# Causal attention: GpSimd takes up to 9 of 16 tiles of exponentials into a partial sum, and rows of constants are loaded where they are used

## The chip, the cores and the metric

One Trainium2 chip, one core. The metric is the device time of one execution in microseconds. The kernel is one program that runs two transformer layers: about twenty phases one after the other, each ending in a barrier of all engines.

## What is computed

```
x = x + L0_xattn(layernorm(x), ctx)      # 16 heads of 16, keys: 1601 rows of ctx
x = x + L0_ffn(layernorm(x))             # 32 experts, capacity 80, and 16 small adapters
x = x + L1_xattn(layernorm(x), ctx)
x = x + L1_ffn(layernorm(x))             # 16 experts, top 4, and 2 shared ones

L1_xattn:  x = ln1(xx);  x = x + mha(x, x, causal=True);  x = ln2(x);  x = x + mha(x, ctx, causal=False)

mha(x, y): q, k, v = projections of ln(x), ln(y), ln(y)         # 16 heads of 32, 2048 queries
    a = softmax(q k^T / sqrt(32))
    if causal:  a = a * (t > s)          # key t, query s: AFTER the softmax, later keys are kept
    x_out = x + (a v) li1_w + li1_b
    return x_out + gelu(ln(x_out) li2_w + li2_b) li3_w + li3_b
```

Since the mask is applied after the softmax, every key counts in the divisor, but only keys later than the query count in the values.

## The kernel before, in words

`program` runs the phases in order: `load_constants` (all small constants, among them `rows`, 2832 numbers that are broadcast to the 128 partitions by one DMA), `ctx_block`, `layernorm`, `attention`, `project_out`, router and experts of the first layer, then the second layer: `layernorm` (twice with a gain and an offset from `rows`), `attention_stacked` (the causal one, `a1`, and later the one over ctx, `a2`), `project_out`, `gelu_ffn`, and at the end `half_rows`, `gate1`, `route` and `moe`. The profile writes both attentions of the second layer with the same names (`a_e`, `a_pd`); they are told apart by time: the tile loop of the causal one runs from about 1378 to 2340 us of the span, that of the other from about 2650 to 3444.

`attention_stacked` goes over 4 groups of 4 heads and, in each, over 4 chunks `qc` of 512 queries: 16 chunks `n`. In a chunk it goes over tiles `kt` of 128 keys (16 in a1, 13 in a2). In a1 the tiles with `kt < 4 qc` are "passed": all their keys are earlier than the queries, so they only need the sum of exponentials, which ScalarE accumulates (L1031). The others are active: 16, 12, 8 and 4 in the four chunks. The first four active tiles (`i` = 0 to 3) are the diagonal ones. For each tile and each of the 4 heads:

- TensorE computes the scores (`score`, L1185 or L1182) into one of 3 PSUM tiles `sc`;
- ScalarE writes the exponentials `e` (L1034) into a ring of `ering` buffers, 3 in a1 and 4 in a2;
- in a diagonal tile GpSimd multiplies one 128x128 block per head by the mask, into `em` (L992), and `po` waits for it (`masked`);
- TensorE adds the values into `po` (`sum_values`, L1208, L1211, L1212) and, by a matmul with ones, the divisors into `pd` (`sum_weights`, L1229). Each f32 matmul is two instructions in the profile, so the 4 heads of a tile are 8.

TensorE runs a tile behind: in iteration m it does scores 0 and 1 of tile m, `sum_values` of tile m-1, scores 2 and 3 of tile m, `sum_weights` of tile m-1. Between these steps it puts "units" of the next chunk (`some_work`): 64 matmuls for the row maxima, which VectorE reduces (L1154, L1082, three PSUM tiles `wb` in turn), projections of q, k and v, and the division of the chunk before. The number of units by step is fixed in advance, in proportion to `TILE_WORK` 8 and `PASSED_WORK` 5.

In a2, GpSimd adds 8 of the 13 tiles of exponentials of a chunk (L999) into `part_sum`, cleared at the start of the chunk by a memset (L982); TensorE leaves out `pd` for those and adds `part_sum` by one such matmul set at the last tile (L1226). ScalarE doesn't write a buffer of the ring before GpSimd has added what was in it (`part_added`). In a1 GpSimd only makes `em`.

Engines take their instructions in order. The SP queue issues nearly all DMAs. At the end of `half_rows` it issues 16 loads for `wall` (L2006), the weights of the routed experts, that `moe` uses; the phase doesn't wait for them. In `gate1` VectorE starts with a memset and then the sum of the scores and `gate_bias` (L1927); `route` begins with the store of `meta` (L2124), which the phase waits for.

Of the kernel before, what the change touches and what calls it, by code (L numbers as in the profile page):

```python
# [100 lines left out]
def load_constants(nc, a, cols, rows, ident, ones, x_sb):  # L101
    ctx, sb, ps, sem = phase(nc, "init")
    with ctx:
# [20 lines left out]
def layernorm(nc, name, src, dst, rows, width, affine=None, outs=(), ident=None):  # L124
# [6 lines left out]
    with ctx:  # L131
# [4 lines left out]
        eps = sb("eps", [P, 1])  # L136
        tp = ps("tp", [P, 4, CH]) if outs else None
# [6 lines left out]
        groups = [(k, t0, min(t0 + TPC, n)) for t0 in range(0, n, TPC) for k in range(nk)]  # L144

        @block.vector
        def _(dve):
# [8 lines left out]
            if affine is not None:  # L156

                dve.wait_ge(var_ready, n)
                for t in range(n):
                    dve.scalar_tensor_tensor(out=dst[:, t, :], in0=src[:, t, :], scalar=mv[:, t, 0:1], in1=affine[0],  # L160
                                             op0=ALU.subtract, op1=ALU.mult).then_inc(scaled, 1)
# [4 lines left out]
            for t in range(n):  # L166
# [4 lines left out]
                else:  # L171
                    dve.wait_ge(scaled, t + 1)
                    dve.scalar_tensor_tensor(out=dst[:, t, :], in0=dst[:, t, :], scalar=rstd[:, t:t + 1], in1=affine[1],
# [623 lines left out]
def attention_stacked(nc, a, name, wq, wk, wv, xq, nkq, xk, nkk, nkeys, scale, causal, ot, ones, bq=None, bk=None, bv=None, ering=4, ones_at=None):  # L797
# [57 lines left out]
    for m in range(nkt * NC):  # L855
# [3 lines left out]
    shared = [[kt for kt in range(1, nkt - 2) if kt % 4 and own_sum and not causal]  # L859
              for n in range(NC)]  # L860
# [10 lines left out]
    for n in range(NC):  # L871
# [12 lines left out]
        during.append(work)  # L884
    after = [(u, n) for n in (NC - 2, NC - 1) for u in ("divisors", "divide")]
# [4 lines left out]
    with ctx:  # L890
# [10 lines left out]
        part_sum = sb("part_sum", [P, HG, CH]) if own_sum and not causal else None  # L901
# [23 lines left out]
        o_taken, inverse_spread, part_added, part_cleared = sem("o_taken"), sem("inverse_spread"), sem("part_added"), sem("part_cleared")  # L925
# [41 lines left out]
        def _(pool):  # L967
# [9 lines left out]
            for n in range(NC if causal or own_sum else 0):  # L977
# [3 lines left out]
                if not causal:  # L981
                    pool.memset(part_sum[:, :, :], 0.0).then_inc(part_cleared, 1)  # L982
                    pool.wait_ge(part_cleared, n + 1)
                for kt in range(nkt):
# [9 lines left out]
                    if kt in shared[n]:  # L994
                        m = nshared[n] + shared[n].index(kt)
                        pool.wait_ge(exp_done, HG * (nkt * n + kt + 1))
                        if m:
                            pool.wait_ge(part_added, m)
                        pool.tensor_tensor(part_sum[:, :, :], part_sum[:, :, :], e[:, (nkt * n + kt) % ering, :, :],  # L999
                                           ALU.add).then_inc(part_added, 1)  # L1000

        @block.scalar
        def _(act):
# [10 lines left out]
            for m in range(nkt * NC):  # L1014
                r = kt_rows[m % nkt]
                for j in range(HG):
                    act.wait_ge(sc_ready, HG * m + j + 1)

                    if m >= ering:
# [3 lines left out]
                        if kt in shared[n]:  # L1023
                            act.wait_ge(part_added, nshared[n] + shared[n].index(kt) + 1)
# [95 lines left out]
        def _(pe):  # L1120
# [67 lines left out]
            def sum_values(n, kt):  # L1188
# [14 lines left out]
                for j in range(HG):  # L1203
# [8 lines left out]
                    pe.matmul(po[h:h + SLOT, P * i:P * i + P], w, em[:r, kt % 2, j, :], start=(i == 0), stop=stop)  # L1212
# [3 lines left out]
            def sum_weights(n, kt):  # L1216
# [5 lines left out]
                if kt == nkt - 1 and not causal:  # L1222
                    pe.wait_ge(part_added, nshared[n + 1])
# [8 lines left out]

            for u in before:
# [6 lines left out]
            shares = [1, 1, 1, 1, 1, 1 if own_sum else 0]  # L1240
            tile_work = [PASSED_WORK if passed(m // nkt, m % nkt) else TILE_WORK for m in range(nkt * NC + 1)]
            for m in range(nkt * NC + 1):
                n, kt = m // nkt, m % nkt
                ahead = (m + LEAD) // nkt
                window = range(max(nkt * ahead - LEAD, 0), min(nkt * (ahead + 1) - LEAD, nkt * NC + 1))
                work = during[ahead] if ahead < NC else []
                in_all = sum(shares) * sum(tile_work[k] for k in window)

                def some_work(step):

                    before_tile = sum(shares) * sum(tile_work[k] for k in range(window.start, m))
                    lo, hi = (-(-len(work) * (before_tile + tile_work[m] * sum(shares[:i])) // in_all) for i in (step, step + 1))
                    for u in work[lo:hi]:
                        unit(u)

# [3 lines left out]
                for half in range(2):  # L1259
                    if n < NC:  # L1260
                        score(n, kt, 2 * half)
                    some_work(3 * half)
                    if n < NC:
                        score(n, kt, 2 * half + 1)
                    some_work(3 * half + 1)
# [4 lines left out]
                    some_work(3 * half + 2)  # L1270
# [4 lines left out]
def project_out(nc, name, ot, wo_dram, bias, res, dst):  # L1275

    ctx, sb, ps, sem = phase(nc, name)
    with ctx:
        wo = sb("wo", [P, NG, D])
        y = [ps(f"y{i}", [P, D]) for i in range(4)]  # L1280
        w_loaded, y_ready, summed, biased = sem("w_loaded"), sem("y_ready"), sem("summed"), sem("biased")
        block = ctx.enter_context(nc.Block())

        @block.sync
        def _(sp):
            sp.dma_start(wo[:, :, :], wo_dram).then_inc(w_loaded, 16)

# [17 lines left out]
        def _(pool):  # L1305
            for t in range(NT):
                pool.wait_ge(summed, t + 1)
                pool.tensor_tensor(dst[:, t, :], dst[:, t, :], bias, ALU.add).then_inc(biased, 1)


def gelu_ffn(nc, a, name, xt, w2_dram, w3_dram, b2, b3, xo, adds, dst, halved):
# [9 lines left out]
    with ctx:  # L1321
        w2 = sb("w2", [P, KC, FF])
        w3 = sb("w3", [P, nj, D])
# [1394 lines left out]
```

## Time and profile before

| | us |
|---|---|
| time, median of 3 runs | 4138.86 (4130.42 to 4160.15) |
| time of the profiled execution | 4170.53 |
| its span | 4168.8 |
| busy: TensorE matmul | 3451.8 (83%) |
| busy: VectorE | 2533.2 (61%) |
| busy: ScalarE | 1936.3 (46%) |
| busy: GpSimd | 1257.1 (30%) |
| mean granted clock of TensorE | 0.899 |

Times in the rows are microseconds from the start of the span unless marked ns. A row of a timeline is an instruction or a run of equal ones: start, length, engine, line, operation, output <- inputs, count, and in brackets the idle time before it and what ended that. PE is TensorE, PEld its weight loads, DVE VectorE, ACT ScalarE, POOL GpSimd, SPq the queue of SyncE. Averages over the whole span hide the stages: the two attention loops of the second layer, 1756 us of it, are another matter than the phases between them.

### The profile page before, as it was taken

The page shows a single profiled execution, that of the slowest core. Times are in us where ns is not written, and L with a number is a line of the kernel's source. Part 1 is how long each engine was busy: PE and PEld are TensorE (multiplying, and loading weights), DVE is VectorE, ACT ScalarE, POOL GpSimd, SP SyncE. Part 2 cuts the span into 40 slices and gives each one's busy share as a digit, 9 for nine tenths or more (in the row PEclk, how much of TensorE's full clock was granted, in tenths as well). Part 3 has the DMA queues.
Part 4 walks back from the last instruction along what each step waited for, and adds up shares of the span by engine and source line. Part 5 has one row for each costly group of instructions (what it writes and reads, how often), then busy time and mean ns, then how long its engine had stood idle before and what let it go on. Part 6 is the DMA issues. An engine that isn't in the chain of part 4 may idle for free. (4 is left out here: it accounts for less than half of the span.)

```text
span 4168.8 us, 66056 instructions
## 1 busy us (share of the span) xinstructions
PE 3451.8 (83%) x23063; PEld 1585.2 (38%) x23063; DVE 2533.2 (61%) x4809; ACT 1936.3 (46%) x3897; POOL 1257.1 (30%) x658
## 2 busy tenths in 40 slices
PE   4999999518855999999999773899999994838997
PEld 1333333307752232333322442233333323526775
DVE  4777774481135777687776245777777744344564
ACT  1677777001101456565666361355555561512442
POOL 2000000102211000010000161377777783524454
PEclk7999999758876999999999786899999996968998
DMA  1000000336641000000000061100000001562445
GB/s 59 10 16 10 11 7 3 102 118 208 223 150 38 21 8 16 14 11 19 9 6 4 6 193 50 24 11 21 10 21 9 9 1 54 185 245 82 89 83 116
DMA packets 174222, 236.69 MB, mean 57 GB/s; under 512 B 36499, under 2 KB 148442, under 8 KB 166874
## 3 DMA queue, kind: packets, MB, share of 16 engines
q1 hardware_dynamic: 154858, 207.81, 15.9%
q0 software_dynamic: 19056, 24.88, 3.3%
q8 instruction: 179, 2.93, 0.3%
q14 instruction: 129, 1.06, 0.1%
HBM read 136.16 MB, written 66.82 MB: 49 GB/s over the span
## 5 line engine op out<-in xcount | busy, mean ns | idle before, releaser
L1082 DVE TENSOR_REDUCE a_part_max<-a_wb 128x1 f32<-128x512 f32 (+1 forms) x2048 | 1168.3, 626 | 300.7 <-PE a_wb L1154 291.6
L1034 ACT ACTIVATE a_e<-a_sc 128x512 f32<-128x512 f32 (+1 forms) x1472 | 798.1, 598 | 803.3 <-PE a_sc L1185 800.2
L1154 PE MATMUL a_wb<-a_ks,a_qs 96*128 96x512 f16 (+1 forms) x2048 | 746.2, 372 | 48.4 <-DMA a_qs<-a_stage 28.0
L999 POOL TENSOR_TENSOR a_part_sum<-a_part_sum,a_e 128x2048 f32<-128x2048 f32 x128 | 581.4, 4542 | 141.2 <-ACT a_e L1034 78.0
L1185 PE MATMUL a_sc<-a_qs,a_ks 97*128 97x512 f16 (+1 forms) x1472 | 546.0, 384 | 12.9 <-DMA a_qs<-a_neg_max 8.1
L607 DVE TENSOR_REDUCE xa_part_max<-xa_mx 128x2 f32<-128x802 f32 x512 | 472.1, 986 | 131.3 <-PE xa_mx L711 128.3
L543 ACT ACTIVATE xa_e<-xa_sc 128x512 f32<-128x512 f32 (+1 forms) x832 | 445.6, 596 | 128.0 <-PE xa_sc L698 120.4
L1154 PEld LDWEIGHTS a_wb<-a_ks,a_qs 96*128 96x128 f16 x2048 | 200.0, 98 | 657.3 <-DVE a_part_max L1082 473.3
L992 POOL TENSOR_TENSOR a_em<-a_e,a_later 128x512 f32<-128x512 f32 x64 | 81.1, 1267 | 955.1 <-ACT a_e L1034 944.9
L1208 PE MATMUL a_po<-a_e,a_v 128*32 128x512 f32 (+1 forms) x2432 | 323.9, 605 | 1.8 <-ACT a_dc L1012 1.0
L734 PE MATMUL xa_po<-xa_e,xa_v 128*32 128x256 f32 (+1 forms) x3328 | 269.6, 396 | 7.5 <-ACT xa_oc L593 2.6
L1229 PE MATMUL a_pd<-a_e,ones 128*32 128x512 f32 (+1 forms) x1920 | 257.9, 609 | 0.0
L1031 ACT ACTIVATE a_e<-a_sc 128x512 f32<-128x512 f32 x384 | 223.4, 648 | 28.3 <-PE a_sc L1182 27.4
L1185 PEld LDWEIGHTS a_sc<-a_qs,a_ks 97*128 97x128 f16 (+1 forms) x1472 | 145.0, 100 | 204.7 <-ACT a_e L1034 87.2
L711 PE MATMUL xa_mx<-xa_khi,xa_qhi 32*128 32x401 f16 x1024 | 180.7, 352 | 18.5 <-DVE xa_part_max L607 13.9
L2288 POOL DMA_INDIRECT routed_sums<-moe_ye,moe_ids x79 | 139.3, 1763 | 164.9 <-DVE moe_ye L2427 119.2
L698 PE MATMUL xa_sc<-xa_qs,xa_ks 49*128 49x512 f16 (+1 forms) x832 | 177.2, 394 | 12.2 <-DMA xa_qs<-xa_neg_max 12.2
L2327 PE MATMUL moe_g<-wall,moe_xt 128*128 (+1 forms) x666 | 173.1, 317 | 1.5 <-ACT moe_xt L2379 0.8
L2327 PE MATMUL moe_up<-wall,moe_xt 128*128 (+1 forms) x666 | 171.5, 316 | 1.6 <-issue 1.6
L1182 PE MATMUL a_sc<-a_ks,a_qs 97*128 97x512 f16 x384 | 146.6, 404 | 7.4 <-ACT a_e L1031 6.6
L2346 PE MATMUL moe_y<-wall,moe_ht 128*128 (+1 forms) x999 | 129.2, 275 | 26.9 <-DVE moe_ht L2405 26.3
L2395 DVE TENSOR_TENSOR moe_hf<-moe_sg,moe_up 128x352 f32<-128x352 f32 x111 | 57.9, 521 | 136.9 <-ACT moe_sg L2367 111.7
(348 smaller groups left out, 4458.2 us busy)
## 6 DMA issues: line engine op xcount, KB each, us to landing
experts_w_up<-in_we SPq DMA_DIRECT2D x32, 1024.0 KB, 7.1
a_ffn_stage<-in_wm SPq DMA_DIRECT2D x72, 272.0 KB, 3.5
expert_halves<-a_ffn_cut SPq DMA_DIRECT2D x72, 272.0 KB, 3.1
wall<-expert_halves SPq DMA_DIRECT2D x18, 1088.0 KB, 19.4
experts_w_down<-in_we SPq DMA_DIRECT2D x32, 512.0 KB
a_qs<-a_stage SPq DMA_DIRECT2D x384, 32.0 KB, 1.8
moe_xr<-sorted_rows SPq DMA_DIRECT2D x79, 136.5 KB
a_ks<-a_stage SPq DMA_DIRECT2D x336, 32.0 KB, 1.8
```

The lines of the kernel that those rows point to most:

```text
L543: act.activation(e[:r, m % ering, j, :], src[:r, :], ACT.Exp, scale=scale).then_inc(s_taken, 1)
L607: dve.tensor_reduce(part_max[:, 2 * h:2 * h + 2, t, c], src[:, :, :mxw], AX.X, ALU.max).then_inc(m_taken, 1)
L734: last = pe.matmul(po[h:h + SLOT, q], w, e[:r, m % ering, j, q], start=(kt == first and part == 0), stop=stop)
L999: pool.tensor_tensor(part_sum[:, :, :], part_sum[:, :, :], e[:, (nkt * n + kt) % ering, :, :], ALU.add).then_inc(part_added, 1)
L1031: act.activation(e[:, m % ering, j, :], sc[(HG * m + j) % NSC][:, :], ACT.Exp, scale=scale, accum_out=span_sum[:, n % 2, t, j, c:c + 1]).t ...
L1034: act.activation(e[:r, m % ering, j, :], sc[(HG * m + j) % NSC][:r, :], ACT.Exp, scale=scale).then_inc(exp_done, 1)
L1082: dve.tensor_reduce(part_max[:, j, t, k:k + 1], src[:, :mxw], AX.X, ALU.max).then_inc(unit_taken, 1)
L1154: last = pe.matmul(dst[:, :mxw], qs[:STACK, j, n % NQ, P * t:P * t + P], ks[:STACK, g % 2, j, mxs[k]:mxs[k] + mxw], start=True, stop=True)
L1185: pe.matmul(sc[i % NSC][:r, :], ks[:STACK + 1, n // NCH % 2, j, P * kt:P * kt + r], qs[:STACK + 1, j, n % NQ, :], start=True, stop=True).t ...
L1208: last = pe.matmul(po[h:h + SLOT, :], w, e[:r, m % ering, j, :], start=(kt == first), stop=stop)
L1229: last = pe.matmul(pd[h:h + SLOT, :], ones[:r, :SLOT], e[:r, m % ering, j, :], start=(kt == first), stop=(kt == nkt - 1))
L2327: last = pe.matmul(dst[:, :], xt[j % 2][:, px, k, :], weights(u, pw, off + EI * k, EI), start=(k == 0 and px == 0 and pw == 0), stop=(k == ...
```

## The change

Four things:

- In a1 GpSimd also adds tiles of exponentials: those active tiles with `i > 0`, `i % 3 != 0` and `kt < nkt - 2`, in chunks with more than 4 active tiles. This is 9, 6, 4 and 0 tiles in the four chunks of a group, 76 in all. TensorE leaves out `pd` for them and adds `part_sum` once in each of the 12 chunks that have any. The ring in a1 stays at 3 buffers. In program order GpSimd makes the mask of a tile first and then adds that tile.
- In both attentions the memset of `part_sum` goes: the first shared tile of a chunk is copied, not added. The tiles of a2 are the same as before.
- To make room for `part_sum` in a1, `rows` no longer stays in SBUF. Each phase that needs a part of it loads it itself, on SP: `ctx_block` (bv, waited for at its end), `layernorm` with a gain, `project_out`, `gelu_ffn` (behind w2 and w3), `gate1`.
- `some_work` is rewritten (`work_at`) and gives each step the same units as before.

```diff
+def row_of(a, n):
+    o, k = ROWS[n]
+    return a["rows"][:, o:o + k].partition_broadcast(P).rearrange("p o n -> p (o n)")
...
-            sp.dma_start(rows[:, :], a["rows"].partition_broadcast(P).rearrange("p o n -> p (o n)")).then_inc(loaded, 16)
             sp.dma_start(x_sb[:, :, :], a["x"].rearrange("o (t p) d -> p (o t) d", p=P)).then_inc(loaded, 16)
-            sp.wait_ge(loaded, 48)
+            sp.wait_ge(loaded, 32)
...
+        if affine is not None:
+            @block.sync
+            def _(sp):
+                for i in range(2):
+                    sp.dma_start(gains[i][:, :], affine[i]).then_inc(gains_loaded, 16)
...
                 dve.wait_ge(var_ready, n)
+                dve.wait_ge(gains_loaded, 32)
...
-    shared = [[kt for kt in range(1, nkt - 2) if kt % 4 and own_sum and not causal]
-              for n in range(NC)]
+    def adds_up(n, kt):
+
+        i = kt - (TPC * (n % NCH) if causal else 0)
+        active = nkt - (kt - i)
+        return own_sum and active > TPC and 0 < i and kt < nkt - 2 and (i % 3 != 0 if causal else kt % 4 != 0)
+
+    shared = [[kt for kt in range(nkt) if adds_up(n, kt)] for n in range(NC)]
...
-                if not causal:
-                    pool.memset(part_sum[:, :, :], 0.0).then_inc(part_cleared, 1)
-                    pool.wait_ge(part_cleared, n + 1)
...
                         pool.wait_ge(exp_done, HG * (nkt * n + kt + 1))
+                        tile = e[:, (nkt * n + kt) % ering, :, :]
                         if m:
-                            pool.wait_ge(part_added, m)
-                        pool.tensor_tensor(part_sum[:, :, :], part_sum[:, :, :], e[:, (nkt * n + kt) % ering, :, :],
-                                           ALU.add).then_inc(part_added, 1)
+                            pool.wait_ge(pool_added, m)
+                        if kt == shared[n][0]:
+                            pool.tensor_copy(part_sum[:, :, :], tile).then_inc(pool_added, 1)
+                        else:
+                            pool.tensor_tensor(part_sum[:, :, :], part_sum[:, :, :], tile, ALU.add).then_inc(pool_added, 1)
...
-                if kt == nkt - 1 and not causal:
-                    pe.wait_ge(part_added, nshared[n + 1])
+                if kt == nkt - 1 and shared[n]:
+                    pe.wait_ge(pool_added, nshared[n + 1])
                     for j in range(HG):
                         h = SLOT * j
                         pe.matmul(pd[h:h + SLOT, :], ones[:, :SLOT], part_sum[:, j, :], start=False, stop=False)
...
             sp.dma_start(wo[:, :, :], wo_dram).then_inc(w_loaded, 16)
+            sp.dma_start(bias[:, :], bias_dram).then_inc(bias_loaded, 16)
...
             sp.dma_start(w2[:, :, :], w2_dram).then_inc(w2_loaded, 16)
             sp.dma_start(w3[:, :, :], w3_dram).then_inc(w3_loaded, 16)
+            sp.dma_start(b3[:, :], b3_dram).then_inc(b3_loaded, 16)
...
+        @block.sync
+        def _(sp):
+            sp.dma_start(gate_bias[:, :], bias_dram).then_inc(bias_loaded, 16)
...
             dve.wait_ge(iota_ready, 2)
-            link(dve.tensor_tensor(sfc[:, :, :], sco[:, :, :], gate_bias.unsqueeze(1).to_broadcast([P, NT, E1]), ALU.add))
+            dve.wait_ge(bias_loaded, 16)
+            link(dve.tensor_tensor(sfc[:, :, :], sco[:, :, :], gate_bias[:, :].unsqueeze(1).to_broadcast([P, NT, E1]), ALU.add))
...
             sp.dma_start(ct[:, 0, :], a["ctx_t"]).then_inc(loaded, 16)
-            sp.wait_ge(loaded, 16)
+            sp.dma_start(bv[:, :], row_of(a, "bv0")).then_inc(loaded, 16)
+            sp.wait_ge(loaded, 32)
```

## Rows read from the trace of the kernel before

**Rows 1.** Busy time by stretch: span and length, each engine's busy us, granted clock, DMA.

```profile
1624.50:1695.40 70.90, 69.28 (x438) 20.30 (x437) 47.58 (x78) 36.26 (x72) 4.58 (x4) 1.00 0.08 22
1763.30:1818.00 54.70, 52.55 (x308) 16.87 (x306) 46.33 (x79) 37.43 (x100) 5.06 (x4) 1.00 0.03 8
```

**Rows 2.** Timeline, one plain tile of a 16-tile chunk of the causal attention.

```profile
1645.54 1.06 PE L1229 MATMUL a_pd<-a_e,ones 128*32 128x512 f32 x8
1646.54 0.39 PE L1185 MATMUL a_sc<-a_qs,a_ks 97*128 97x512 f16 x1
...
1647.51 1.06 PE L1208 MATMUL a_po<-a_e,a_v 128*32 128x512 f32 x8
...
1649.15 1.09 ACT L1034 ACTIVATE a_e<-a_sc 128x512 f32<-128x512 f32 x2 [1.11 <-PE a_sc L1185]
...
1651.45 1.06 PE L1208 MATMUL a_po<-a_e,a_v 128*32 128x512 f32 x8
```

**Rows 3.** Groups by line and shape (busy us, mean ns): causal loop, then the other.

```profile
L1082 DVE TENSOR_REDUCE a_part_max<-a_wb 128x1 f32<-128x512 f32 x960 | 606.7, 685 | 149.4 <-PE a_wb L1154 145.5
...
L1082 DVE TENSOR_REDUCE a_part_max<-a_wb 128x1 f32<-128x401 f32 x960 | 492.0, 568 | 125.1 <-PE a_wb L1154 120.6
```

**Rows 4.** Groups by line, whole span: what operations cost on GpSimd.

```profile
L999 POOL TENSOR_TENSOR a_part_sum<-a_part_sum,a_e 128x2048 f32<-128x2048 f32 x128 | 581.4, 4542 | 141.2 <-ACT a_e L1034 78.0 <-issue 49.1 <-POOL a_part_sum L999 0.4
...
L982 POOL MEMSET a_part_sum<- 128x2048 f32 x16 | 28.9, 1806 | 104.8 <-PE a_pd L1229 104.7
L1374 POOL TENSOR_TENSOR a_xo<-a_xo,x 128x4096 f32<-128x4096 f32 x3 | 27.8, 9256 | 45.6 <-POOLq L2616 27.2 <-POOLq L131 18.4
...
L485 POOL CAST xa_qhi<-xa_raw 128x512 f16<-128x512 f32 x16 | 9.8, 611 | 428.5 <-ACT xa_raw L555 421.1 <-DMA xa_ks<-xa_khi 7.4
```

**Rows 5.** Timeline, diagonal tiles: a 16-tile chunk, then one of 8 active tiles.

```profile
1629.03 1.27 POOL L992 TENSOR_TENSOR a_em<-a_e,a_later 128x512 f32<-128x512 f32 x1 [3.76 <-ACT a_e L1034]
...
1632.85 1.27 POOL L992 TENSOR_TENSOR a_em<-a_e,a_later 128x512 f32<-128x512 f32 x1 [2.55 <-ACT a_e L1034]
...
1638.70 0.87 PE L1211 MATMUL a_po<-a_e,a_v 128*32 128x384 f32 x8
...
1790.51 1.27 POOL L992 TENSOR_TENSOR a_em<-a_e,a_later 128x512 f32<-128x512 f32 x1 [2.55 <-ACT a_e L1034]
...
1796.11 0.88 PE L1211 MATMUL a_po<-a_e,a_v 128*32 128x384 f32 x8
```

**Rows 6.** Timeline, the last chunk of the second attention.

```profile
3404.95 37.26 POOL L999 TENSOR_TENSOR a_part_sum<-a_part_sum,a_e 128x2048 f32<-128x2048 f32 x8 [2.04 <-issue]
...
3442.26 1.06 PE L1226 MATMUL a_pd<-a_part_sum,ones 128*32 128x512 f32 x8 [3.51 <-POOL a_part_sum L999]
```

**Rows 7.** DMA issues: count, KB each, median us from issue to landing.

```profile
x<-token_sums SPq DMA_DIRECT2D x2, 2048.0 KB, 8.5
...
x<-in_x SPq DMA_DIRECT2D x1, 2048.0 KB, 12.5
...
ct<-in_ctx_t SPq DMA_DIRECT2D x1, 800.5 KB, 4.2
```

**Rows 8.** Around gate1: SP's issues, VectorE's first use of gate_bias, DMA load, one landing.

```profile
3676.70 20.38 SPq L2006 DMA_DIRECT2D wall<-expert_halves  x16
...
3698.44 0.43 DVE L1927 TENSOR_TENSOR gate_sfc<-m_sco,rows 128x256 f32<-128x256 f32 x1 [0.59 <-POOL meta L1920]
...
3714.94 0.37 SPq L2124 DMA_DIRECT2D token_halves<-meta  x1
3726.80 104.51 SPq L2249 DMA_DIRECT2D moe_xr<-token_halves  x16
...
3720.00:3721.00 1.00, 0.00 (x0) 0.00 (x0) 0.93 (x8) 0.00 (x0) 0.00 (x0) 0.50 1.00 418
3722.00:3723.00 1.00, 0.00 (x0) 0.00 (x0) 0.86 (x5) 0.00 (x0) 0.00 (x0) 0.50 0.97 62
...
token_halves<-meta SPq DMA_DIRECT2D x1, 136.0 KB, 10.9
```

More of the change, by code:

```diff
@@ L98, in phase, with load_constants @@
     return ctx, sb, ps, sem
-def load_constants(nc, a, cols, rows, ident, ones, x_sb):
+def row_of(a, n):
+    o, k = ROWS[n]
+    return a["rows"][:, o:o + k].partition_broadcast(P).rearrange("p o n -> p (o n)")
+def load_constants(nc, a, cols, ident, ones, x_sb):
     ctx, sb, ps, sem = phase(nc, "init")
@@ L136, in layernorm @@
         eps = sb("eps", [P, 1])
+        gains = [sb(f"gain{i}", [P, width]) for i in range(2)] if affine is not None else None
+        gains_loaded = sem("gains_loaded")
         tp = ps("tp", [P, 4, CH]) if outs else None
@@ L884, in attention_stacked, with work_at @@
         during.append(work)
+    shares = [1, 1, 1, 1, 1, 1 if own_sum else 0]
+    tile_work = [PASSED_WORK if passed(m // nkt, m % nkt) else TILE_WORK for m in range(nkt * NC + 1)]
+    def work_at(m, step):
+        ahead = (m + LEAD) // nkt
+        window = range(max(nkt * ahead - LEAD, 0), min(nkt * (ahead + 1) - LEAD, nkt * NC + 1))
+        work = during[ahead] if ahead < NC else []
+        in_all = sum(shares) * sum(tile_work[k] for k in window)
+        before_tile = sum(shares) * sum(tile_work[k] for k in range(window.start, m))
+        lo, hi = (-(-len(work) * (before_tile + tile_work[m] * sum(shares[:i])) // in_all) for i in (step, step + 1))
+        return work[lo:hi]
     after = [(u, n) for n in (NC - 2, NC - 1) for u in ("divisors", "divide")]
@@ L900, in attention_stacked @@
         later = sb("later", [P, P]) if causal else None
-        part_sum = sb("part_sum", [P, HG, CH]) if own_sum and not causal else None
+        part_sum = sb("part_sum", [P, HG, CH]) if own_sum else None
         part_max = sb("part_max", [P, HG, TPC, nmx])
@@ L1023, in _ @@
                         if kt in shared[n]:
-                            act.wait_ge(part_added, nshared[n] + shared[n].index(kt) + 1)
+                            act.wait_ge(pool_added, nshared[n] + shared[n].index(kt) + 1)
                     n, kt = m // nkt, m % nkt
@@ L1211, in sum_values @@
                         pe.matmul(po[h:h + SLOT, :P * i], w, e[:r, m % ering, j, :P * i], start=False, stop=False)
-                    pe.matmul(po[h:h + SLOT, P * i:P * i + P], w, em[:r, kt % 2, j, :], start=(i == 0), stop=stop)
+                    last = pe.matmul(po[h:h + SLOT, P * i:P * i + P], w, em[:r, kt % 2, j, :], start=(i == 0), stop=stop)
                 if not own_sum or kt in shared[n]:
@@ L1231, in sum_weights, with some_work @@
                 last.then_inc(pv_done, 1)
+            def some_work(m, step):
+                for u in work_at(m, step):
+                    unit(u)
             for u in before:
@@ L1269, in _, with project_out @@
                         sum_weights((m - 1) // nkt, (m - 1) % nkt)
[L1270 removed]
+                    some_work(m, 3 * half + 2)
             for u in after:
                 unit(u)
[L1275 removed]
+def project_out(nc, name, ot, wo_dram, bias_dram, res, dst):
     ctx, sb, ps, sem = phase(nc, name)
@@ L1305, in _, with gelu_ffn @@
         def _(pool):
+            pool.wait_ge(bias_loaded, 16)
             for t in range(NT):
                 pool.wait_ge(summed, t + 1)
-                pool.tensor_tensor(dst[:, t, :], dst[:, t, :], bias, ALU.add).then_inc(biased, 1)
-def gelu_ffn(nc, a, name, xt, w2_dram, w3_dram, b2, b3, xo, adds, dst, halved):
+                pool.tensor_tensor(dst[:, t, :], dst[:, t, :], bias[:, :], ALU.add).then_inc(biased, 1)
+def gelu_ffn(nc, a, name, xt, w2_dram, w3_dram, b2, b3_dram, xo, adds, dst, halved):
     ctx, sb, ps, sem = phase(nc, name)
@@ L1892, in _, with gate1 @@
             pair(NP - 1, last=True)
-def gate1(nc, a, sco, gate_bias, meta):
+def gate1(nc, a, sco, bias_dram, meta):
     ctx, sb, ps, sem = phase(nc, "gate1")
@@ L2482, in program @@
         a["ident"] = ident
-        load_constants(nc, a, cols, rows, ident, ones, x)
+        load_constants(nc, a, cols, ident, ones, x)
         def col(n):
@@ L2487, in col @@
             return cols[:, o:o + k]
-        def row(n):
-            o, k = ROWS[n]
-            return rows[:, o:o + k]
         def scope():
@@ L2595, in program, with ctx_block @@
                 half_rows(nc, a, x, sco, wall, wall_in, half_ident, before, every, ident)
-                gate1(nc, a, sco, row("gate_bias"), meta)
+                gate1(nc, a, sco, row_of(a, "gate_bias"), meta)
             route(nc, a, meta, slots, tile_e, before, every)
             moe(nc, a, wall, wall_in, slots, tile_e, half_ident, x, out)
-def ctx_block(nc, a, name, ct):
+def ctx_block(nc, a, name, ct, bv):
     ctx, sb, ps, sem = phase(nc, name)
```

49 lines of the change are left out of this document (22 added, 27 removed).

## The prediction

> **What bounds the kernel now.** I read the page first (shares, then the chain, which covers only the tail of the program), then busy time by stretch, then the timeline of single tiles. [Rows 1] cut one head group of the causal attention into its chunks of 512 queries: in the chunk with 16 active tiles TensorE is busy 69.3 of 70.9 us, in the one with 8 it is 52.6 of 54.7, at a granted clock of 1.00 (the 2.4 GHz level), while VectorE is at 47.6 and 46.3 and GpSimd at 4.6 and 5.1. So TensorE sets the pace, and GpSimd is idle. VectorE is the next bound: 46.3 of 54.7 us in the chunk with 8 active tiles.
>
> [Rows 2] show one steady tile: the two value sums (po) stand 3.94 us apart (1647.51, 1651.45), packed with matmuls. The divisor sum (pd) begins at 1645.54 and the next matmul at 1646.54: a pd costs 1.00 us of TensorE. The tile's last exponential ends at 1649.15 + 1.09 = 1650.24, and po for it begins at 1651.45. Without the pd between them po would begin at 1650.45, 0.2 us after the exponential: just enough. So a dropped pd is worth its full 1.00 us in a plain tile.
>
> **What is removed and added in the causal attention.** By the new rule GpSimd takes 9, 6, 4 and 0 tiles of a group's four chunks, 19 per group, 76 in all. Removed: 76 pd. Added: a sum over part_sum in 12 chunks, 1.00 us each. Naively 76 - 12 = 64 us. Two things take from this.
>
> Plain tiles (diagonal index i of 4 or more): 7, 4 and 2 per group, 52 in all. Every three tiles hold two adds of 4.54 us [rows 4], 9.1 us of GpSimd, against 3 x 3.94 - 2 x 1.00 = 9.8 us of TensorE. The ring of three exponential buffers gives an add until about half a microsecond into the third tile after its own. The second add of a pair begins at latest 4.5 us after the first and ends 9.1 us after the first pair's exponential, about 1.5 us before its buffer is wanted. VectorE needs 4 to 5 reductions of 0.685 us at most a tile [rows 3], 2.7 to 3.4 us, against 2.9 to 3.0 us of TensorE in a shared tile; the three work buffers and the unshared tile between take up that excess. I give these 52 tiles 1.00 us each: -52.
>
> Diagonal tiles (i = 0 to 3): here GpSimd also makes em, the masked block, and po waits for it. GpSimd works in order, so the mask of tile 3 queues behind the add of tile 2. In [rows 5] mask 2 of a 16-tile chunk begins at 1632.85, as soon as its exponentials are done; the pd of tile 1 comes after these, so its removal makes nothing earlier. Then: mask 1.27, add 4.54, mask 1.27, some 0.1 of signals: po of tile 3 not before 1632.85 + 7.2 = 1640.05. Before it began at 1638.70. So up to po 3 nothing is gained from the two dropped pd and 1.35 us are lost. The chunk with 8 active tiles: 1790.51 + 7.2 = 1797.7 against 1796.11, a loss of 1.6; I take 1.6 for the 12-tile chunk too. Four groups: 4 x (1.35 + 1.6 + 1.6) = 18. After po 3 everything follows from it.
>
> Causal attention: -52 + 12 + 18 = -22 us.
>
> The first operation of a chunk is a copy of 128x2048, not an add. No such row exists. Bounds: the memset of the same tile, 1.81 us, and the add, 4.54; nearest is the cast of 128x512, 0.61, four times that is 2.4 [rows 4]. I take 2.2. Mask 1 begins at 1629.03 and ends at 1630.30, so the copy ends at 1632.5, before mask 2 wants GpSimd at 1632.85: free. Any longer copy delays mask 2 one to one; at 4.54 it is 2.0 us late, in 12 chunks 24 us. The Trainium skill (GPSIMD Engine Reference, Engine selection) has one-input operations at roughly line rate and two-input ones about twice slower, by which the copy is hidden; no row here shows that copy.
>
> **Second attention.** Memset and its wait go, and the first add becomes a copy. Only the last chunk, which has no maxima to compute, waits for GpSimd: its adds start at 3404.95, when the second tile's exponentials are ready, run without a gap, and the sum over part_sum follows at 3442.26 [rows 6]. The memset was done before; the copy saves 4.54 - 2.2 = 2.3 us. -2.4 with the small waits for it (0 to -5).
>
> **Rows of constants.** At the start x lands 12.5 us after its issue, queued with the 1416 KB of constants. The same 2048 KB alone took 8.5 us [rows 7]: -4.0. The next block gains 256 KB for bv beside the 800.5 KB of ct (4.2 us): at that rate at most +1.3, taken as +1. The layernorm gains are loaded under 16 statistics instructions, the output biases behind the weights that TensorE waits for longer, b3 under the first full-width add on GpSimd, 9.26 us [rows 4]: nothing, and if a cover were gone, about 2 us each.
>
> The gate's bias is another matter. It is issued on SP at the start of gate1, and SP has just issued 16 transfers for wall, one expert each [rows 8]. These are still running: 418 GB/s with the DMA engines full until 3721, then 62 GB/s at 3722. The precedent is meta, 136 KB, issued at 3714.94: it landed 10.9 us later, at 3725.8, and small packets appear only when the large ones have ended. So this queue works in order, and 16 numbers per partition issued at about 3697.9 land at about 3722.5. VectorE's first instruction that wants them ran at 3698.44: +24 us (23 to 26). Behind it lie the whole gate chain and route, up to the first loads of moe at 3726.80; the chain from meta to there is VectorE's, so it isn't shortened by meta now landing sooner. The Trainium skill (DMA: Bandwidth & Descriptors, Queues, rings and completion order) says that each DMA engine consumes a ring's descriptors in order; the rows of meta agree.
>
> **Sum.** -22 - 2.4 - 3 + 24 = -3.4 us. The profiled execution took 4170.53 us (span 4168.8), 0.8% above the median of 4138.86; the stages concerned are the same, so I take the difference over: 4138.86 - 3.4 = 4135 us.
>
> **Rivals.**
> - The bias isn't held up (it lands within 2 us, as if on a queue of its own): +1.4 in place of +24, so 4113 us. For it: the transfer is tiny. Against: meta.
> - The diagonal costs nothing and all 64 us come: 4135 - 42 = 4093 us, faster by 1.1%. It would need a mask that isn't behind an add; the program order of GpSimd says otherwise.
> - The copy is as slow as an add: +24 from mask 2, 4159 us. For it: no row of a copy. Against: the cast.
> - Slower: GpSimd becomes the bound through the ring of three. With an add of a us, a pair of shared tiles costs 2a in place of 9.8 from a = 4.9 on, 26 pairs, and the diagonal 12 x (a - 4.54). At a = 5.9 this is 26 x 2.0 + 12 x 1.36 = 68 us: 4203 us; slower by 1% from a = 5.5. Against: in the second attention 128 adds beside a busy VectorE held 4.54 us, and VectorE's reductions there took 0.568 us for 401 columns, in the causal one 0.685 for 512 [rows 3], the same per column within 6%. The Trainium skill (GPSIMD Engine Reference, Key points) names contention with VectorE instructions that have two SBUF inputs; this rival is that rule, and the rows of VectorE here are nearly all reductions from PSUM.
>
> **How the numbers follow.** Forecast 0.62, bias free 0.10, all 64 us 0.06, slow copy 0.13, slow add 0.05, the rest 0.04 for small effects either way. The range reaches from the free bias with a few microseconds more to the slow copy with as many: 4105 to 4168. About 1%, 41 us, is what a measurement can tell from no change: faster 0.06, same 0.89, slower 0.05. The chief claim is that two effects of some 25 us cancel.
>
> **What would show it.** In the causal chunks: a gap on TensorE before po of tile 3 with GpSimd's mask as its releaser, mask 3 beginning 5.8 us after mask 2; tile steps of 2.95 us where pd is gone; adds of 4.5 us; a copy of 1.8 to 2.5 us. Chunks of 16 active tiles shorter by some 5 us, of 12 by 1, of 8 longer by 0.6. In gate1: VectorE waiting some 24 us for the DMA of gate_bias. At the start: statistics 3 us earlier. The forecast is wrong if the bias lands at once, if TensorE waits for exponentials after the dropped pd (margin 0.2 us), or if the clock falls below 1.00 after the gaps at tile 3.

## The result, and the profile after

The changed kernel takes 4217.98 us (median of 4 runs, 4208.73 to 4239.58), the kernel before in the same comparison 4137.43: a ratio of 1.019, 95% interval 1.015 to 1.023, that is 80.5 us slower. I had forecast 4135 us, no change. The profiled execution of the changed kernel has a span of 4207.0 us, at a mean granted clock of 0.889.

The path can be cut where `a_dc`, the copy of a chunk's divisors, starts: once per chunk, 16 per attention. View of one tile (`a_dc`), in a window for each attention; the columns are count, duration in ns (least, median, greatest), first and last start in us. The kernel before:

```profile
L1012 ACT ACTIVATE a_dc<-a_pd x16: 591/591/592, 1450.3 to 2340.4; 128x512 f32<-128x512 f32 x16
L1012 ACT ACTIVATE a_dc<-a_pd x16: 591/591/592, 2705.2 to 3451.1; 128x512 f32<-128x512 f32 x16
```

The changed kernel:

```profile
L1044 ACT ACTIVATE a_dc<-a_pd x16: 592/592/592, 1435.1 to 2322.1; 128x512 f32<-128x512 f32 x16
L1044 ACT ACTIVATE a_dc<-a_pd x16: 592/592/593, 2686.2 to 3500.6; 128x512 f32<-128x512 f32 x16
```

| stretch | before | after | change | forecast |
|---|---|---|---|---|
| to the first row maximum of the causal attention | 1310.6 | 1301.7 | -8.9 | -3 |
| causal attention, to its last `a_dc` | 1029.8 | 1020.4 | -9.4 | -22 |
| from there to the first `a_dc` of the second attention | 364.8 | 364.1 | -0.7 | 0 |
| second attention, first to last `a_dc` | 745.9 | 814.4 | +68.5 | -2.4 |
| last `a_dc` to the store of `meta` (L2124, now L2160) | 263.8 | 287.5 | +23.6 | +24 |
| from there to the end of the span | 453.9 | 419.0 | -34.8 | 0 |

The last row is not the change. Between its first and last transposition on TensorE, `moe` took 399.4 us in the trace of the kernel before, 365.0 in that of the changed one, and 364.8 to 366.9 in those of all ten experiments, one of them (e2) with the gate and the loads untouched. So it was a stall in the one profiled execution of before, which took 4170.53 us while the median is 4137. Likewise the first row moves by more than the change explains: it lies between 1296.5 and 1331.4 in these traces; of its 8.9 us, 3.5 are there at the first normalised tile. Without both, the stretches give -3.5 - 9.4 - 0.7 + 68.5 + 23.6 = +78.5 us, against +80.5 between the medians.

**Second attention.** Busy time by stretch, first to last `a_dc` (columns as in [rows 1]), before and then after:

```profile
2705.20:3451.10 745.90, 719.37 (x4338) 231.21 (x4336) 511.83 (x1009) 431.70 (x808) 571.84 (x135) 0.99 0.05 11
```

```profile
2686.20:3500.60 814.40, 748.58 (x4338) 240.93 (x4336) 566.34 (x1009) 433.40 (x808) 503.58 (x120) 0.96 0.04 10
```

The same 4338 matmuls; VectorE's time grew by 54.5 us with the same 1009 instructions. The copy that spreads the inverse divisors over 512 columns (`a_spread`, one per chunk) explains it. The tile view of it, second attention, last chunks left out, after:

```profile
L1129 DVE COPY a_spread<-a_inverse x14: 4099/4486/4494, 2695.3 to 3411.0; 128x512 f32<-128x512 f32 x14
```

Before it was 427 to 455 ns. The timelines show why. The changed kernel, GpSimd, then VectorE, then TensorE:

```profile
2690.92 1.89 POOL L1030 COPY a_part_sum<-a_e 128x2048 f32<-128x2048 f32 x1 [14.17 <-ACT a_e L1066]
2694.99 4.52 POOL L1032 TENSOR_TENSOR a_part_sum<-a_part_sum,a_e 128x2048 f32<-128x2048 f32 x1 [2.17 <-ACT a_e L1066]
...
2695.29 4.49 DVE L1129 COPY a_spread<-a_inverse 128x512 f32<-128x512 f32 x1
2699.71 1.52 DVE L1114 TENSOR_REDUCE a_part_max<-a_wb 128x1 f32<-128x401 f32 x3
...
2700.33 0.52 PE L1186 MATMUL a_wb<-a_ks,a_qs 96*128 96x401 f16 x1 [3.07 <-DVE a_part_max L1114]
```

The kernel before, same chunk:

```profile
2709.94 9.21 POOL L999 TENSOR_TENSOR a_part_sum<-a_part_sum,a_e 128x2048 f32<-128x2048 f32 x2 [3.37 <-issue]
...
2714.30 0.45 DVE L1097 COPY a_spread<-a_inverse 128x512 f32<-128x512 f32 x1
```

In the kernel before the copy came 4.36 us after the first add had begun, at its end. Now GpSimd's first operation is a copy of 1.89 us, so the second tile's add can begin as soon as its exponentials are there, 0.30 us ahead of VectorE's copy, and the copy ends 0.27 us after the add. Meanwhile the three work buffers of the maxima fill, and TensorE stands still for 3.07 us. The view of TensorE's waits over the loop and some us more, after (us in total, times, longest):

```profile
PE a_wb L1186 <- DVE a_part_max L1114: 42.8, 20, 3.4
```

It was 1.6 before. After such a gap the clock falls. Busy time by stretch of 4 us, after:

```profile
2690.00:2694.00 4.00, 4.00 (x27) 1.22 (x26) 3.13 (x7) 2.06 (x5) 1.89 (x1) 1.00 0.15 35
2694.00:2698.00 4.00, 3.25 (x23) 1.37 (x21) 3.63 (x4) 2.59 (x5) 3.01 (x1) 1.00 0.19 46
2698.00:2702.00 4.00, 1.67 (x6) 0.95 (x7) 4.00 (x6) 0.60 (x1) 1.52 (x2) 0.75 0.10 26
2702.00:2706.00 4.00, 4.00 (x24) 2.07 (x24) 2.13 (x5) 1.51 (x3) 4.00 (x1) 0.83 0.01 2
2706.00:2710.00 4.00, 4.00 (x27) 0.97 (x25) 3.73 (x8) 2.73 (x6) 0.61 (x2) 1.00 0.00 0
```

A granted clock of 0.75 or 0.83 is a mean of 1.2 and 2.4 GHz. So the 68.5 us are 29 us more for the same matmuls (748.6 - 719.4) and 39 us more in which TensorE stands still (65.8 against 26.5): the waits for maxima grew by 41 (42.8 - 1.6), some others shrank.

VectorE's copy is held in the same way, for less time, in the trace of the kernel before. A chunk of the causal attention, GpSimd making a mask, then VectorE:

```profile
1460.84 1.27 POOL L992 TENSOR_TENSOR a_em<-a_e,a_later 128x512 f32<-128x512 f32 x1 [67.86 <-ACT a_e L1034]
...
1461.56 0.83 DVE L1097 COPY a_spread<-a_inverse 128x512 f32<-128x512 f32 x1
```

Here, and in two chunks more, the copy begins 0.72 us into a mask and takes 0.83 us, to 0.28 us after the mask's end.

**Causal attention.** The diagonal went as forecast. Timeline of a 16-tile chunk, changed kernel (against [rows 5]):

```profile
1618.08 1.27 POOL L1021 TENSOR_TENSOR a_em<-a_e,a_later 128x512 f32<-128x512 f32 x1 [0.72 <-ACT a_e L1066]
1619.30 4.52 POOL L1032 TENSOR_TENSOR a_part_sum<-a_part_sum,a_e 128x2048 f32<-128x2048 f32 x1
1623.77 1.45 POOL L1021 TENSOR_TENSOR a_em<-a_e,a_later 128x512 f32<-128x512 f32 x1
...
1625.37 1.53 PE L1243 MATMUL a_po<-a_e,a_v 128*32 128x384 f32 x8 [2.56 <-POOL a_em L1021]
```

`po` of tile 3 begins 7.29 us after mask 2 (forecast 7.2), mask 3 5.7 us after it (5.8). Over the causal loop TensorE waits for masks:

```profile
PE a_po L1243 <- POOL a_em L1021: 42.5, 27, 2.7
```

against 2.6 us at this line before (L1211). What I had not priced is what follows the gap of 2.56 us:

```profile
1621.00:1625.00 4.00, 1.81 (x13) 1.16 (x11) 3.50 (x7) 2.12 (x4) 4.00 (x2) 0.97 0.19 49
1625.00:1629.00 4.00, 3.63 (x20) 1.19 (x20) 0.94 (x2) 0.60 (x1) 0.22 (x1) 0.50 0.16 43
1629.00:1633.00 4.00, 4.00 (x21) 1.63 (x20) 1.74 (x3) 1.68 (x3) 3.14 (x1) 0.67 0.00 0
1633.00:1637.00 4.00, 4.00 (x27) 1.06 (x26) 2.92 (x5) 2.06 (x4) 2.69 (x2) 1.00 0.00 0
```

0.50 is 1.2 GHz. TensorE's busy time over the causal attention fell from 973.9 to 924.1 us, by 50 and not by the 64 of the dropped matmuls, and its mean granted clock there from 0.96 to 0.94. Chunk by chunk after the first (from one `a_dc` to the next), those of 16 active tiles came out 2.2 to 3.5 us shorter (forecast some 5), those of 12 between 1.7 shorter and 1.3 longer (forecast 1 shorter), those of 8 longer by 0.6 to 2.3 (forecast 0.6).

**The gate.** Timeline of SP and VectorE, changed kernel, and, of its DMA issues, KB and us to landing:

```profile
3725.68 20.34 SPq L2042 DMA_DIRECT2D wall<-expert_halves  x16
3746.51 1.81 SPq L1949 DMA_DIRECT2D gate_gate_bias<-in_rows  x1
...
3771.49 0.42 DVE L1963 TENSOR_TENSOR gate_sfc<-m_sco,gate_gate_bias 128x256 f32<-128x256 f32 x1 [24.71 <-DMA gate_gate_bias<-in_rows]
```

```profile
gate_gate_bias<-in_rows SPq DMA_DIRECT2D x1, 8.0 KB, 24.9
```

8 KB took 24.9 us to land, behind 16 transfers, and VectorE waited 24.71 us. From the first of the 16 issues to VectorE's sum: 21.7 us before [rows 8], 45.8 now, +24.1.

### The profile page after: what moved, and what is told of

Read it like the earlier page. It is cut to its first block and busy times, and to the rows that moved or that the text cites. A ratio compares the mean times of both kernels' runs of the same rounds, so it can differ in the third digit from the quotient of the medians.

```text
span 4207.0 us, 65463 instructions
## 1 busy us (share of the span) xinstructions
PE 3424.6 (81%) x22551; PEld 1590.6 (38%) x22551; DVE 2582.1 (61%) x4809; ACT 1934.3 (46%) x3897; POOL 1494.7 (36%) x718
## 5 line engine op out<-in xcount | busy, mean ns | idle before, releaser
L1032 POOL TENSOR_TENSOR a_part_sum<-a_part_sum,a_e 128x2048 f32<-128x2048 f32 x176 | 796.5, 4525 | 206.4 <-ACT a_e L1066 193.4
L1217 PE MATMUL a_sc<-a_qs,a_ks 97*128 97x512 f16 (+1 forms) x1472 | 556.1, 391 | 11.9 <-DMA a_qs<-a_neg_max 8.0
L1261 PE MATMUL a_pd<-a_e,ones 128*32 128x512 f32 (+1 forms) x1312 | 181.9, 627 | 0.0
L499 POOL CAST xa_qhi<-xa_raw 128x512 f16<-128x512 f32 x16 | 9.8, 610 | 427.9 <-ACT xa_raw L569 420.6
L1030 POOL COPY a_part_sum<-a_e 128x2048 f32<-128x2048 f32 x28 | 52.9, 1890 | 251.4 <-ACT a_e L1066 243.9
```

Of the source, the lines that this page charges most:

```text
L1032: pool.tensor_tensor(part_sum[:, :, :], part_sum[:, :, :], tile, ALU.add).then_inc(pool_added, 1)
L1217: pe.matmul(sc[i % NSC][:r, :], ks[:STACK + 1, n // NCH % 2, j, P * kt:P * kt + r], qs[:STACK + 1, j, n % NQ, :], start=True, stop=True).t ...
L1261: last = pe.matmul(pd[h:h + SLOT, :], ones[:r, :SLOT], e[:r, m % ering, j, :], start=(kt == first), stop=(kt == nkt - 1))
```

## The experiments

Theory A: VectorE's spreading copy is held by a GpSimd add that has begun before it, until that add ends, and the shorter first operation on GpSimd brought this about. Rivals: something else lengthens the second attention (B), GpSimd holds any VectorE instruction with SBUF on both sides (C), or the copy is slow under GpSimd work wherever it begins (H). Theory D: the gate's bias stands behind 16 transfers; rival E: `moe` gives that back. Theory F: the add ahead of mask 3 is what costs the causal attention its gain; rival G: the gain is only moved. All ratios are to the kernel before, run beside each; its median there lies between 4130.64 and 4137.43 us, so a difference between two experiments that were not run together is good to some 7 us.

**e1_a2_memset.** The changed kernel with GpSimd's second attention as before:

```diff
+                if not causal:
+                    pool.memset(part_sum[:, :, :], 0.0).then_inc(part_cleared, 1)
+                    pool.wait_ge(part_cleared, n + 1)
...
-                        if kt == shared[n][0]:
+                        if causal and kt == shared[n][0]:
```

> The changed kernel, but in the second attention GpSimd clears the partial sum and adds its first tile, as in the kernel before. Theory A (in the changed kernel VectorE's copy that spreads the inverse divisors, L1129, starts 0.3 us after a GpSimd add has begun and is held until it ends, 4.35 us instead of 0.44, because the first operation of a chunk is now 1.89 us long instead of 4.5): the copy falls back into the end of the first add and takes 0.45 us, the second attention is 794 us long again instead of some 850, and the kernel takes 4218 - 55 = about 4163 us. Rival B (something else lengthens the second attention: a lower clock, the layout of memory, the sharing in the first attention that precedes it): within 10 us of 4218 us.

Measured: 4144.59 us, ratio 1.002 (0.999 to 1.005): 73 us less than the changed kernel, and 18 less than expected. The second attention's loop takes 748.9 us, 65.5 less, where I had counted only the 55 us of the copies; one of its 16 copies is still held (4.47 us, the others about 0.43). B falls.

**e2_before_copy.** The converse, on the kernel before:

```diff
-                if not causal:
-                    pool.memset(part_sum[:, :, :], 0.0).then_inc(part_cleared, 1)
-                    pool.wait_ge(part_cleared, n + 1)
...
+                        if kt == shared[n][0]:
+                            pool.tensor_copy(part_sum[:, :, :], tile).then_inc(part_added, 1)
+                        else:
```

> The kernel before, with one edit: in the second attention the clearing and first add of the partial sum become a copy. Nothing else of the change. Theory A: this alone moves VectorE's spreading copy under a GpSimd add; it takes over 4 us in 14 chunks and the kernel takes 4137 + 55 = about 4192 us. Rival B: no slower than before, or 2 us faster as I forecast for this part.

Measured: 4201.22 us, ratio 1.016 (1.012 to 1.020), +67 us, 9 more than expected, from 16 GpSimd operations that became 2.65 us shorter each (4.54 to 1.89) and 16 memsets that went. Loop 814.5 us. In this kernel and window:

```profile
L1097 DVE COPY a_spread<-a_inverse x14: 4099/4483/4490, 2712.7 to 3428.2; 128x512 f32<-128x512 f32 x14
```

**e5_spread_reduce.** The changed kernel, with the copy written as a reduction over an axis of length 1:

```diff
-                    dve.tensor_copy(spread[:, :, :, :], inverse[:, :, :].unsqueeze(3).to_broadcast([P, TPC, HG, SLOT])).then_inc(
+                    dve.tensor_reduce(spread[:, :, :, :].rearrange("p t j d -> p (t j) d"),
+                                      inverse[:, :, :].rearrange("p t j -> p (t j)").unsqueeze(2).unsqueeze(3).to_broadcast([P, TPC * HG, SLOT, 1]), AX.X, ALU.max).then_inc(
```

> The changed kernel; the spreading of the inverse divisors stays on VectorE, at the same place, with the same SBUF source and the same 512 numbers written per partition, but as a reduction over an axis of length 1 instead of a copy. GpSimd's work is untouched. Theory A2 (what is held is the copy form; the copy at 427 ns for 512 numbers, 0.83 ns each, is faster than VectorE's reductions at 1.33 ns each, so it runs in a faster mode, and that mode waits for GpSimd): the reduction takes 0.6 to 0.8 us even when a GpSimd add is running, and the kernel takes 4218 - 66 = about 4152 us. Rival C (any VectorE instruction that both reads and writes SBUF is held by a GpSimd add): over 4 us in 14 chunks, and the time stays at 4218.

Measured: 4153.11 us, ratio 1.003 (1.000 to 1.006), 65 us less than the changed kernel. Timeline of it, GpSimd and VectorE:

```profile
2708.74 9.21 POOL L1032 TENSOR_TENSOR a_part_sum<-a_part_sum,a_e 128x2048 f32<-128x2048 f32 x2 [2.17 <-ACT a_e L1066]
...
2709.05 0.69 DVE L1129 TENSOR_REDUCE a_spread<-a_inverse 128x512 f32<-128x512 f32 x1
```

It begins 0.31 us after the add, as the copy did, moves the same bytes, and takes 0.69 us. C falls: what is held is the faster form. The Trainium skill (SBUF — State Buffer, Who interferes with whom) says just this: VectorE's copies can enter a mode that uses the pair of ports it shares with GpSimd, whoever starts first has that pair for its whole instruction, and a reduction on Trainium2 never contends. The traces agree, with 4.49 against 0.69 us.

**e3_spread_recip.** The changed kernel, with one reciprocal in place of the small one and the copy:

```diff
-                    dve.reciprocal(inverse[:, :, :], den).then_inc(unit_taken, 1)
-                    dve.wait_ge(unit_taken, i + 1)
-                    dve.tensor_copy(spread[:, :, :, :], inverse[:, :, :].unsqueeze(3).to_broadcast([P, TPC, HG, SLOT])).then_inc(
-                        inverse_spread, 1)
+                    dve.reciprocal(spread[:, :, :, :], den.unsqueeze(3).to_broadcast([P, TPC, HG, SLOT])).then_inc(inverse_spread, 1)
+                    dve.wait_ge(inverse_spread, n + 1)
+                    dve.sem_inc(unit_taken, 1)
```

> The changed kernel; VectorE makes the spread inverse divisors with one reciprocal that reads the divisors (in PSUM in the second attention) 32 times over and writes 512 numbers, so the copy from SBUF to SBUF (a_spread from a_inverse) is gone. GpSimd's work stays as it is. Theory A (the hold is a matter of that copy's form): the reciprocal isn't held, 0.6 to 1.2 us, the second attention is back at some 795 us, and the kernel takes 4218 - 55 = about 4163 us. Rival C (anything that VectorE runs against a GpSimd add of two operands is held there): the reciprocal takes over 4 us and the time stays at 4218.

Measured: 4252.96 us, ratio 1.030 (1.024 to 1.035), 35 us more than the changed kernel. A miss, but not in C's favour:

```profile
L1127 DVE RECIPROCAL a_spread<-a_wb x20: 3356/3357/3359, 1447.6 to 3545.6; 128x512 f32<-128x512 f32 x20
L1127 DVE RECIPROCAL a_spread<-a_total x12: 3352/3353/3354, 1518.0 to 2380.3; 128x512 f32<-128x512 f32 x12
```

A reciprocal of 512 numbers costs 3.36 us wherever it stands, from PSUM or SBUF, with or without an add beside it: nothing waits, it is slow, 6.6 ns for a number against 1.3 for the reduction. I had guessed 0.6 to 1.2. It does show that the harm needs no hold by GpSimd, only a VectorE instruction of this length: the second attention's loop is 800.6 us, in line with the table below, and the causal one, where the copy was hardly held, is 54 us longer. One thing more differs there: the long instruction itself reads the divisors' work buffer in the second attention, so that buffer comes free later too.

**e9_divisors_2_later, e10_divisors_4_later.** The changed kernel with the divisors' units 2 and 4 places later in the second attention (e9; e10 has 30 in place of 28):

```diff
-            work[26:26], work[32:32] = [("divisors", n - 1)], [("divide", n - 1)]
+            at = 26 if causal else 28
+            work[at:at], work[at + 6:at + 6] = [("divisors", n - 1)], [("divide", n - 1)]
```

> The changed kernel; in the second attention the two units that make the divisors and the division stand 2 places later in TensorE's and VectorE's order of units, each place about 0.72 us (50 us for some 70 units). In the changed kernel the spreading copy begins 0.30 us (or 0.64) after a GpSimd add of 4.52 us has begun and lasts 4.49 us (or 4.17): in both cases it ends 0.27 us after the add. Theory A (it is held until the add that runs ends): begun 1.4 us later it lasts about 3.0 us, VectorE loses 20 us less in 14 chunks, and by the 66 us that 55 us of hold were worth (e1, e5) the kernel takes about 4218 - 24 = 4194 us. Rival H (the copy is slow under any GpSimd activity, by a factor of ten, wherever in the add it begins): still over 4 us, 4218.

> As e9, 4 places later: the copy begins some 3.2 us into the add. Theory A: it lasts 1.3 to 1.9 us, and the kernel takes about 4218 - 48 = 4170 us. Rival H: over 4 us, 4218. If the shift carries the copy past the end of the add into the next one, single copies of over 4 us remain and the time lies between.

Measured: 4196.09 us (ratio 1.016, 1.012 to 1.021) and 4177.45 us (1.011, 1.007 to 1.014). A pair of timeline rows of e9, then of e10:

```profile
2690.69 9.17 POOL L1033 TENSOR_TENSOR a_part_sum<-a_part_sum,a_e 128x2048 f32<-128x2048 f32 x2 [2.17 <-ACT a_e L1067]
2691.80 3.69 DVE L1130 COPY a_spread<-a_inverse 128x512 f32<-128x512 f32 x1
```

```profile
2720.96 9.18 POOL L1033 TENSOR_TENSOR a_part_sum<-a_part_sum,a_e 128x2048 f32<-128x2048 f32 x2 [2.17 <-ACT a_e L1067]
2723.72 2.05 DVE L1130 COPY a_spread<-a_inverse 128x512 f32<-128x512 f32 x1
```

Start after the add's start plus length: 1.11 + 3.69 = 4.80; 2.76 + 2.05 = 4.81; in the changed kernel 0.30 + 4.49 = 4.79 and 0.64 + 4.17 = 4.81; in the kernel before 4.36 + 0.45 = 4.81. Over all 14 chunks of each of these traces, a copy that begins up to 4.38 us into the add ends 4.79 to 4.82 us after the add's start, about 0.28 after its end. H falls. The dose and its effect, second attention, first to last `a_dc`, always 4338 matmuls:

| kernel | `a_spread`, mean us | VectorE busy | TensorE busy | its waits for maxima | loop |
|---|---|---|---|---|---|
| before | 0.44 | 511.8 | 719.4 | 1.3 | 745.9 |
| e5 | 0.69 | 515.3 | 721.4 | 1.6 | 746.2 |
| e10 | 1.81 | 529.9 | 732.3 | 15.4 | 773.2 |
| e9 | 3.06 | 547.2 | 740.6 | 32.1 | 797.4 |
| changed | 4.35 | 566.3 | 748.6 | 42.5 | 814.4 |

(The means are of the 14 copies inside the loop.) VectorE is far from full in all of them; it is the length of one instruction that matters, against three buffers.

**e4_bias_early.** The changed kernel, with the bias loaded in `half_rows` ahead of the 16 transfers:

```diff
             sp.dma_start(gw[:, :, :], a["gw"]).then_inc(gw_loaded, 16)
+            sp.dma_start(gate_bias[:, :], row_of(a, "gate_bias")).then_inc(bias_loaded, 16)
...
-        @block.sync
-        def _(sp):
-            sp.dma_start(gate_bias[:, :], bias_dram).then_inc(bias_loaded, 16)
```

> The changed kernel; the gate's bias is loaded in the block before gate1, behind the gate's weights and ahead of the 16 transfers of expert weights. Theory D (it stands in the changed kernel behind these 16 transfers on one queue, +24.0 us by the two traces): VectorE's gate chain begins 21.7 us after the first of the 16 is issued instead of 46, and the kernel takes 4218 - 24 = 4194 us. Rival E (the gate's delay is made up in moe, whose stretch was 34 us shorter in the trace of the changed kernel than in that of the kernel before, since the weights have then landed): moe grows by as much as the gate shrinks, and the time stays within 8 us of 4218.

Measured: 4190.73 us, ratio 1.011 (1.007 to 1.015), 27 us less than the changed kernel; `moe` 365.4 us. VectorE's sum of this kernel:

```profile
3770.92 0.42 DVE L1957 TENSOR_TENSOR gate_sfc<-m_sco,gate_bias 128x256 f32<-128x256 f32 x1 [0.62 <-POOL meta L1950]
```

D holds, E falls.

**e6_reduce_bias.** The edits of e5 and e4 together.

> e5_spread_reduce with the gate's bias loaded in the block before gate1 (e4_bias_early's edit). If the two costs are independent: 24 to 27 us less than e5, so about 4127 us, under the kernel before by what the causal sharing and the earlier start bring (9 + 3 us). If the copy is held whatever its form: about 4191 us, as in e4.

Measured: 4125.65 us, ratio 0.996 (0.993 to 0.999), 27 us less than e5: the two costs add up, and without them the change is a small gain.

**e7_no_add_before_mask.** e6 with other shared tiles in the causal attention:

```diff
-        return own_sum and active > TPC and 0 < i and kt < nkt - 2 and (i % 3 != 0 if causal else kt % 4 != 0)
+        return own_sum and active > TPC and 0 < i and kt < nkt - 2 and (i % 3 != 2 if causal else kt % 4 != 0)
```

> e6_reduce_bias with another choice of shared tiles in the causal attention: i % 3 != 2 in place of i % 3 != 0, so 1, 3, 4, 6, 7, 9, 10, 12, 13 and no add of tile 2 stands ahead of the mask of tile 3. Still 9 and 6 tiles in the chunks of 16 and 12 active tiles, 3 in place of 4 in those of 8: 4 divisor sums more. Theory F (the add of tile 2 makes TensorE wait 2.6 us before the value sum of tile 3 in 12 chunks, and these gaps bring the granted clock down, 0.96 against 0.98 in the causal loop): 12 x 2.6 - 4 = 27 us less, and up to 14 more from the clock: 4127 - 27 to - 41, 4086 to 4100 us. Rival G (what is gained ahead of tile 3 is lost behind it, since the adds of tiles 3 and 4 now press on the ring of three buffers): within 8 us of e6.

Measured: 4079.13 us, ratio 0.985 (0.980 to 0.991): 46 us less than e6, 56 less than the kernel before, and below the 4086 to 4100 that I expected. F holds, G falls. The same stretch of a 16-tile chunk, mask 2, mask 3, adds:

```profile
1619.51 1.27 POOL L1021 TENSOR_TENSOR a_em<-a_e,a_later 128x512 f32<-128x512 f32 x1 [0.72 <-ACT a_e L1066]
1623.54 1.26 POOL L1021 TENSOR_TENSOR a_em<-a_e,a_later 128x512 f32<-128x512 f32 x1 [2.77 <-ACT a_e L1066]
1624.76 9.21 POOL L1032 TENSOR_TENSOR a_part_sum<-a_part_sum,a_e 128x2048 f32<-128x2048 f32 x2
```

Mask 3 now waits for its exponentials, not for GpSimd. TensorE's waits for masks at that line fall from 42.0 us to

```profile
PE a_po L1244 <- POOL a_em L1021: 11.6, 15, 1.4
```

and its busy time over the causal attention from 925.8 to 917.2 us although it does 4 more divisor sums. Waits -30, sums +4, and the rest of the matmuls -13 at a mean granted clock of 0.95 against 0.94: -39, and the attention went from 1021.8 to 983.3 us in the traces. The remaining 8 us between the medians are not explained; the runs of one kernel spread by more.

**e8_no_causal_sharing.** e6 without the sharing in the causal attention:

```diff
-        return own_sum and active > TPC and 0 < i and kt < nkt - 2 and (i % 3 != 0 if causal else kt % 4 != 0)
+        return own_sum and not causal and active > TPC and 0 < i and kt < nkt - 2 and (i % 3 != 0 if causal else kt % 4 != 0)
```

> e6_reduce_bias without the sharing in the causal attention: GpSimd only makes the masks there, as in the kernel before. By the two traces the sharing as it is written is worth 9.4 us in the causal attention (64 us less of TensorE's work, 40 us more of waits for masks, 14 us more for the same work at a lower clock), so this kernel is 9 us slower than e6, about 4136 us. If I misread the traces and the sharing gains nothing or costs something, it is as fast as e6 or faster.

Measured: 4126.3 us, ratio 0.998 (0.995 to 1.002), the same as e6 within the intervals. In the traces the causal attention is 1030.2 us against 1021.8, the 8 us expected; the medians don't show them. What can be said is that the sharing as it was written is worth between nothing and some 9 us; the choice of tiles in e7 is worth 46 more.

## Why the prediction was wrong

- **Start, -3:** right, 3.5 us at the first normalised tile.
- **Plain tiles, -52, sums +12, diagonal +18, together -22:** the places and the gaps were right: 64 us less work, and the forecast 18 + 24 = 42 us of waiting ahead of the diagonal `po` came as 42.5 - 2.6 = 40. The step that failed is pricing the rest of the matmuls at the old clock. A gap of some 2.6 us can bring 1.2 GHz for several microseconds after it (0.50 and 0.67 of the clock in the rows above); the matmuls that stayed took 14 us longer in all, so -9.4 and not -22. I had named this among what would make the forecast wrong, but put nothing into the sum or the range for it.
- **Copy on GpSimd, 2.2:** 1.89, ahead of mask 2 in time, as forecast; the rival of a slow copy is out. The adds took 4.52 us, so the rival of a slow add is out too. Out are also a bias that lands at once and all 64 us of the dropped sums.
- **Second attention, -2.4:** this step failed, by 71 us. I asked what becomes of GpSimd's own chain, and only in the last chunk, where somebody waits for it. I did not ask what else on the chip depended on when its adds run. The fact was within reach: the copy `a_spread` took 0.43 us for 512 numbers where a reduction of 512 took 0.685 [rows 3], so it ran in a faster mode; it came at the end of an add; and making the first operation 2.65 us shorter would put the next add in front of it. The hold itself was in the trace too, 0.83 us in place of 0.43 beside a mask. My rival of contention with VectorE was dismissed with "the rows of VectorE here are nearly all reductions from PSUM". "Nearly all" was the fault: the exception is one instruction per chunk, and one of 4.4 us against three buffers is enough. The sentence of the Trainium skill that I cited (GPSIMD Engine Reference, Key points) names VectorE instructions in a two-port mode first, and I weighed it only for those with two SBUF inputs, and only for what they do to GpSimd.
- **Gate, +24:** right, 24.1 between the traces, 27 in e4. That small packet behind 16 transfers was visible in the landing of `meta` [rows 8].
- **Profiled time against the median:** I took the difference over; e2's trace shows `moe` at 365 us with the same gate, so the profile of before held a stall of 34 us of its own. It changed nothing in the sum.

The range of 4105 to 4168 was built from the rivals about GpSimd's price and the bias; none of them held a VectorE instruction that waits for GpSimd. With the two missed terms, -3.4 + 71 + 13 = +81, the sum is what was measured.

## What to carry to other kernels

Before giving GpSimd more work, or only other times for its work, list VectorE's SBUF-to-SBUF copies, with how long after the start of a GpSimd operation each begins; any that starts during one lasted here until about 0.28 us after its end, and a form that isn't a fast copy (here a reduction over an axis of length 1, 0.26 us dearer) was not held here. An engine that is busy 69% of a stretch (511.8 of 745.9 us) can still stop TensorE when one instruction is longer than the buffers in front of it last. Price a gap on TensorE with the slower matmuls behind it, keep a long add from standing ahead of a mask that TensorE waits for, and issue a small load ahead of the big ones of its queue.

## What the runs showed of the hardware that I had not expected

- A VectorE copy of 128x512 that begins 0.30 to 4.38 us into a GpSimd add of 4.52 us ends 4.79 to 4.82 us after the add's start; one that begins 0.72 us into a mask of 1.27 us takes 0.83 us in place of 0.43.
- A gap of 2.56 us on TensorE was followed by 1.2 GHz from about 1625 to 1631 us, and by 2.4 GHz again from 1633 on at full load.
- VectorE's reciprocal takes 3.36 us for 512 numbers and 0.26 for 16; GpSimd copies 128x2048 in 1.89 us, 2.4 times as fast as it adds.
